# Grouping a front stage's small TensorE steps: four groups per chunk between the projection's units, instead of one step after nearly every unit

## What is computed

```python
u = x @ W_in + b_in                       # 8192 x 512 -> 8192 x 1536
uc = _short_conv(u, short_w, short_b)     # three taps along the sequence, per channel
x0, x1, v = jnp.split(uc, 3, axis=-1)
v = v * x1
k = _gen_filter(x.shape[1], W1, b1, f1, W2, b2, f2, W3, b3)   # sin(sin(pe @ W1) @ W2) @ W3, damped
v = _causal_fft_conv(v, k, filter_bias)
y = v * x0
return y @ W_out + b_out
```

## Time and profile before

| | us |
|---|---|
| median of 3 runs | 2255.05 |
| lowest and highest | 2248.68, 2259.68 |
| the profiled execution's own time | 2248.08 |
| its span | 2246.2 |

### The profile page before, as it was taken

How to read it: one execution, slowest core, us unless ns; L and a number is a source line. 1 busy time by engine, 2 the same in 40 slices (tenths; PEclk the granted TensorE clock), 3 DMA queues, 4 the chain that set the end, 5 groups by cost and what they waited for, 6 DMA issues and landing times. The chain is left out here.

```text
span 2246.2 us, 34847 instructions
## 1 busy us (share of the span) xinstructions
PE 1903.8 (85%) x12342; PEld 1293.3 (58%) x12342; DVE 1406.4 (63%) x2748; ACT 933.9 (42%) x1755; POOL 512.1 (23%) x410
## 2 busy tenths in 40 slices
PE   7999999999998799999979999995767586576444
PEld 6777777777776443443458888884636362352000
DVE  5877777877788454554558889884444353364344
ACT  4444444444444344454445555552323242242222
POOL 0100010001000054454445555550302020020000
PEclk9999999999999899999989999997888896697655
DMA  5134233433332577888778877774697999999999
GB/s 166 66 114 141 99 113 113 135 109 112 109 122 102 178 200 232 219 224 245 188 210 243 247 244 233 243 226 185 239 395 289 399 352 406 405 329 411 370 392 344
DMA packets 287298, 513.73 MB, mean 229 GB/s; under 512 B 26480, under 2 KB 105366, under 8 KB 278806
## 3 DMA queue, kind: packets, MB, share of 16 engines
q1 hardware_dynamic: 277909, 494.71, 65.6%
q10 hardware_dynamic: 9216, 16.78, 2.0%
HBM read 309.78 MB, written 201.62 MB: 228 GB/s over the span
## 5 line engine op out<-in xcount | busy, mean ns | idle before, releaser
L90 PE MATMUL p_pu<-p_xT_high,p_win_high 128*128 128x512 f32 (+1 forms) x816 | 330.8, 405 | 14.2 <-DVE p_win_low L85 11.9
L91 PE MATMUL p_pu<-p_xT_high,p_win_low 128*128 128x512 f32 (+1 forms) x816 | 314.4, 385 | 0.0
L92 PE MATMUL p_pu<-p_xT_low,p_win_high 128*128 128x512 f32 (+1 forms) x816 | 314.0, 385 | 0.0
L447 ACT ACTIVATE p_t<-p_pu,p_tbias,p_taps 128x512 f32<-128x512 f32 (+1 forms) x192 | 146.6, 764 | 357.9 <-PE p_pu L92 357.0
L564 DVE SCALAR_TENSOR_TENSOR p_t<-p_pu,p_taps,p_t 128x256 f32<-128x256 f32 (+1 forms) x384 | 208.6, 543 | 6.9
L85 POOL TENSOR_TENSOR p_xT_low<-p_xT,p_xT_high 128x2048 fp32r<-128x2048 f32 (+1 forms) x16 | 71.2, 4448 | 620.1 <-ACT p_xT_high L80 620.1
L849 POOL TENSOR_TENSOR q_y<-q_y 128x512 f32<-128x512 f32 x128 | 160.2, 1271 | 197.4 <-DVE q_y L870 197.4
L90 PEld LDWEIGHTS p_pu<-p_xT_high,p_win_high 128*128 128x128 f32 x816 | 156.4, 192 | 46.7 <-DVE p_xT_low L85 10.0
L92 PEld LDWEIGHTS p_pu<-p_xT_low,p_win_high 128*128 128x128 f32 x816 | 156.0, 191 | 32.8
L91 PEld LDWEIGHTS p_pu<-p_xT_high,p_win_low 128*128 128x128 f32 x816 | 156.4, 192 | 25.4
L1458 PE MATMUL e_pd<-e_taken,e_ff 128*32 128x128 f32 x2048 | 88.4, 329 | 96.0 <-DMA e_ff<-in_L_ffn_f 92.1
(11 more groups left out here) (135 smaller groups left out, 3782.2 us busy)
## 6 DMA issues: line engine op xcount, KB each, us to landing
s_I<-e_out SPq DMA_DIRECT2D x64, 1024.0 KB, 8.2
s_SV<-p_sout SPq DMA_DIRECT2D x128, 256.0 KB, 2.0
q_av<-s_SV SPq DMA_DIRECT2D x64, 512.0 KB, 4.4
s_Z<-q_z SPq DMA_DIRECT2D x128, 256.0 KB, 3.2
o_zin<-s_Z SPq DMA_DIRECT2D x64, 512.0 KB, 4.0
e_ff<-in_L_ffn_f SPq DMA_DIRECT2D x64, 512.0 KB, 9.4
e_inter<-s_I SPq DMA_DIRECT2D x32, 1024.0 KB, 12.3
e_taken<-s_I SPq DMA_DIRECT2D x32, 1024.0 KB, 11.5
```

Source lines behind the costliest of these rows:

```text
L90: pe.matmul(out, a[0], b[0], start=start, stop=False)
L91: pe.matmul(out, a[1], b[0], start=False, stop=False)
L92: return pe.matmul(out, a[0], b[1], start=False, stop=stop)
L447: nc.scalar.activation(t[r][m % 2][:, c], pu[(W + n) % 3][:, c], ACT.Identity, bias=tbias[:, w:w + 1], scale=taps[:, w, 2:3]).then_inc(t_o ...
```

## The change

PE's small steps of a pass no longer follow single units. They come in four groups, after units 2, 5, 8 and 11: two transform steps, one `turn_v`, and in three of the four groups one filter step (`filter_turn` of chunk i - 1 in the first, `filter_in` in the second, `filter_mid` in the fourth). The steps 0 to 5 of chunk i - 1 stand in the second to fourth group of pass i, its steps 6 and 7 in the first group of pass i + 1. On ACT and SP the copies and stores follow at x = 6, 7, 9, 10 and at 0, 1, 3, 4 of the next pass (`copied`). On DVE `angles(i, 0)` moves from x = 0 to x = 6, `angles(i, 1)` from x = 4 to x = 0 of the next pass, `keep_ht` and `keep_hs` to x = 2 of a later pass; on ACT `sine(i, 0)` moves from x = 2 to 8 and `sine(i, 1)` from x = 5 to x = 1 of the next pass, ahead of that place's `keep_s`. `filter_in` gets one more wait, for `ht_ok`. No instruction is added or taken away.

```diff
+        def copied(i, x):
+            ahead, back = {6: 0, 7: 1, 9: 2, 10: 3}, {0: 4, 1: 5, 3: 6, 4: 7}
+            if x in ahead and i >= 1:
+                return (i - 1) * STAGES + ahead[x]
+            return (i - 2) * STAGES + back[x] if x in back and i >= 2 else None
@@ SP
-                    if i and x == 1 and i >= 2:
+                    if x == 4 and i >= 2:
                         store_h(i - 2)
-                    if i and x >= 4:
-                        store_s((i - 1) * STAGES + x - 4)
+                    if copied(i, x) is not None:
+                        store_s(copied(i, x))
...
+            for n in range(NCH * STAGES - 4, NCH * STAGES):
+                store_s(n)
@@ PE, filter_in
                 if i:
                     pe.wait_ge(red2_ok, ONE + i)
+                    pe.wait_ge(ht_ok, ONE + i)
@@ PE
                 for x in range(W):
                     if i < NCH:
                         unit(i + 1, x)
-                        if x == 0:
-                            filter_in(i)
-                        if x == 3:
-                            filter_mid(i)
-                        if x == 7:
-                            filter_turn(i)
-                    m = i * DT + x // 3 - 1
-                    if x % 3 == 2 and 0 <= m < NCH * DT:
-                        turn_v(m)
-                    if i and x >= 4:
-                        stage(i - 1, x - 4)
+                    if x % 3 != 2:
+                        continue
+                    k = x // 3
+                    first = (i - 2) * STAGES + 6 if k == 0 else (i - 1) * STAGES + 2 * k - 2
+                    if first >= 0:
+                        stage(first // STAGES, first % STAGES)
+                        stage(first // STAGES, first % STAGES + 1)
+                    if 0 <= i * DT + k - 1 < NCH * DT:
+                        turn_v(i * DT + k - 1)
+                    if k == 0 and i:
+                        filter_turn(i - 1)
+                    if k == 1 and i < NCH:
+                        filter_in(i)
+                    if k == 3 and i < NCH:
+                        filter_mid(i)
+            for x in (6, 7):
+                stage(NCH - 1, x)
@@ ACT
                     if i < NCH:
                         tap(i, x)
-                        if x == 2:
+                        if x == 8:
                             sine(i, 0)
-                        if x == 5:
-                            sine(i, 1)
...
-                    if i and x >= 5:
-                        keep_s((i - 1) * STAGES + x - 5)
-                    elif i >= 2 and x == 0:
-                        keep_s((i - 1) * STAGES - 1)
-                if i == NCH:
-                    keep_s(NCH * STAGES - 1)
+                    if i and x == 1:
+                        sine(i - 1, 1)
+                    if copied(i, x) is not None:
+                        keep_s(copied(i, x))
+            for n in range(NCH * STAGES - 4, NCH * STAGES):
+                keep_s(n)
@@ DVE
-                if i >= 2:
-                    keep_hs(i - 2)
-                if i == NCH:
-                    break
                 for x in range(W):
-                    taps_add(i, x)
-                    if x % 3 == 2:
-                        gate(i * DT + x // 3)
-                    if x == 0:
-                        angles(i, 0)
-                    if x == 4:
-                        angles(i, 1)
-                    if x == 8:
-                        keep_ht(i)
+                    if i < NCH:
+                        taps_add(i, x)
+                        if x % 3 == 2:
+                            gate(i * DT + x // 3)
+                        if x == 6:
+                            angles(i, 0)
+                    if x == 0 and i >= 1:
+                        angles(i - 1, 1)
+                    if x == 2 and i >= 2:
+                        keep_hs(i - 2)
+                    if x == 2 and i >= 1:
+                        keep_ht(i - 1)
```

## The result

| | median | runs | lowest to highest |
|---|---|---|---|
| before | 2251.12 us | 19 | 2247.0 to 2259.68 |
| after | 2256.38 us | 19 | 2251.42 to 2263.17 |

The ratio is 1.0027, with a 95% interval of 1.0019 to 1.0035: the change costs 4 to 8 us, which is less than the 0.5% that was to count. The profiled execution of the changed kernel took 2260.33 us, with a span of 2258.5 us, where rows 1 gave 2246.2.

A forecast was written before the change was run, and what follows sets the result against it. PE's instructions were taken to bound the front up to about 700 us, then DVE. Terms 0 - 1.0 + 1.5 + 1.2 = +1.7 us on 2255.05 gave 2256.8 us, range 2247 to 2267.

The forecast's parts named there:

- The 0.09 is paid behind the short matmul whatever comes next: On PE, a step's 0.09 us on going out stays whether a unit or another small step follows.
- 8 x 0.00 for the pairs: On PE, putting transform steps in pairs saves nothing: 8 x 0.00 us a chunk.
- The first rival: The 0.09 us belongs to going back to units; seven exits a chunk go, -9.5 us, 2247; chance 0.15.
- The filter steps behind `turn_v` at 0: On PE, filter steps placed behind `turn_v`, a new kind of neighbour, cost 0 us extra.
- `filter_turn` at -0.07: On PE, `filter_turn` behind short transposes takes 0.22 us instead of 0.29: 15 x -0.07 = -1.0 us.
- The meeting of step 7 with the sine: First group of a pass: step 7's copy, behind the sine, allows 6.61 us after unit 0; PE arrives at 6.63.
- The +1.5 us for a bare weight load: Step 7's weight load in the first group is not hidden: 0.1 us, 15 times, +1.5 us.
- The other waits have slack: Mid-front waits other than step 7's are met in time, for example unit 0's additions at 2.7 us, needed at 8.5.
- DVE has 13.5 of 60 us free: In the middle of the front, DVE's 13.5 free us of 60 cover the bursts of additions.
- The end: Last gate at 746.3, 5.0 us earlier; chunk 15's first step 7.6 us later at 753.9 against 752.67: +1.2 us.
- The second: Rival: step 7 waits on the sine chain in every chunk, from 0.75 us each, 11.4 us slower; chance 0.15.
- the third rival: Only the end counts: DVE's waits stay and the clock falls again, +3.7 and up to 3 more, 2261 to 2262; chance 0.12.

The follow-up runs named there:

- experiment 7: Against experiment 4, each pair of transform steps split, one behind the second unit of three, the other behind the third: 2256.81 us, 1.0024 of before.
- experiment 1: Changed kernel with `angles(i, 0)` moved from x = 6 to 8 on DVE and `sine(i, 0)` from 8 to 10 on ACT: 2250.07 us, 0.9992 of before.
- experiment 4: Changed kernel with the filter chain back at its old places on every engine; steps, `turn_v`, copies and stores stay grouped: 2238.74 us, 0.9948 of before.
- experiment 8: The kernel of experiment 4 timed a second time, in another comparison with the kernel before: 2240.76 us, 0.9956 of before.
- Experiment 3: Changed kernel with, in the last pass on ACT, the copy of step 5 of chunk 14 ahead of `sine(15, 1)`: 2253.79 us, 1.0009 of before.
- experiment 5: Kernel before with only the filter chain moved to the changed kernel's places, steps left single: 2263.51 us, 1.0053 of before.
- the four kernels: Before, the changed kernel (1.0027 of before), grouping without the filter chain's move (0.9948), and the filter chain's move with single steps (1.0053).

## Why the prediction was right, and where it was wrong

The forecast, 2256.8 us and no change that counts, met the measured 2256.38. But before's median had moved down from 2255.05 to 2251.12 with more runs. The effect was +1.7 us by the sum and is 4 to 8 us by the ratio, 4.57 in the front by the traces. So that the two times agree within 0.4 us is luck. The direction and "no change that can be told" were right; the terms were not all.

- **"The 0.09 is paid behind the short matmul whatever comes next": wrong for the first step of a group.** The 1.08 us of rows 6 is the distance behind a step that itself follows a step. The *first* step behind a unit goes over in 1.02 to 1.03 us, into a step or into `turn_v` (experiment 7), so it pays 0.02 to 0.03 on going out. One exit in each of four groups is 0.26 us a chunk, about 4 us over 15 chunks, where the sum had 8 x 0.00 for the pairs and 0 for `turn_v` behind a step. The prediction had the number itself: it put step 6 at 1.03 us (T + 5.60 to T + 6.63) and named 1.03 as what would show it, but didn't carry the difference to 1.09 into the sum. The first rival had the sign right, not the size: one exit of a group goes, not all that no longer lead back to a unit.
- **The filter steps behind `turn_v` at 0, and `filter_turn` at -0.07: right.** In the kernel of experiment 1, without recurring waits, the four groups take 2.78, 3.37, 2.55 and 2.98 us from unit to unit: the 2.55 of two steps and `turn_v`, and 0.23 for `filter_turn`, 0.82 for `filter_in`, 0.43 for `filter_mid`. The prediction had 0.22, 0.83 and 0.44. That chunk takes 45.30 us against 45.58.
- **The meeting of step 7 with the sine: right to 0.02 us, its price not paid.** Timelines of ACT and PE, after, for a pass whose unit 0 ends at 438.15:

```profile
443.81 0.42 ACT L485 ACTIVATE p_h<-p_red 128x256 f32<-128x256 f32 x1 [1.61 <-DVE p_red L567]
444.13 0.57 ACT L479 COPY p_sout<-p_ps 128x512 f32<-128x512 f32 x1
...
444.78 1.10 PE L380 MATMUL p_ps<-p_shared,p_dft 128*128 128x512 f32 x2
```

  The sine is at T + 5.66 as forecast, the copy at T + 5.98, step 7 at T + 6.63, with no wait. The +1.5 us for a bare weight load is not there.
- **"The other waits have slack" and "DVE has 13.5 of 60 us free": the step that failed.** A mean over 60 us says nothing of one instruction of 0.29 us that takes 4.55. The hold stood in the trace of before (the rows at 416.70 and 418.47), and I didn't look at what DVE and POOL do at the place to which `angles(i, 0)` moves. It costs 0.46 us a chunk (45.76 against 45.30), 6 us in thirteen chunks. Whether the single wait of 2.4 us in pass 0 costs anything is not shown: experiment 1 has other waits in its place, and the start of the front differs by 1.7 us between two executions of one kernel (the last gate of chunk 0 ends at 74.61 in experiment 4, at 72.90 in experiment 8). The missed terms of the middle are of opposite sign (-0.26 and +0.46 a chunk), which is why the sum still came out near; that too is luck.
- **The end: the mechanism right, its sizes off.** The last gate was put at 746.3 and came at 748.7: the chunk before was 1.8 late at 710.78, where I had 709.0, and DVE took 37.95 to the next gate instead of 37.3, of which 0.5 was a wait for ACT. From the gate to the first step I had 7.6 us and it was 8.3: up to step 7 it is 3.8 (3.9 expected), but from step 7 to the first step of chunk 15 it is 4.5 (3.7 expected), at a granted clock of 0.50 (752 to 757 us). Together the first step came at 757.02, not 753.9: +4.4 against before instead of +1.2. Experiment 3 shows the part of the copy behind the sine in it, 3.6 us up to the first step.
- **Rivals and signs.** The second (the sine holds the first group, more than 0.75 us a chunk) did not arise in the middle. A wait that recurs in each chunk, which I named as what would prove me wrong, did, from another engine. So did a time outside the front that moved by more than 2 us (7.7), though only in the two profiled executions. Of the third rival the clock did fall, to 0.50 from 752 to 759 us, but DVE's waits did not stay. I had also called the filter chain's move nearly free, and by the four kernels it costs 12 to 18 us. What I judged neutral was one half that wins half a per cent and one that loses more.

## What to carry to other kernels

A change with two parts is costed, and if possible timed, as two: here a gain of 12 us and a loss of 18 were shipped together and looked like nothing. Where an instruction is moved to another place in a queue, look at that place in the trace for what the *other* engines do in those microseconds, above all GpSimd when VectorE's work moves; busy shares won't show it. And what ends a software pipeline has to be read apart: work that is put off into the next pass can be free in the middle and stands uncovered after the last pass, here 7.1 us from the last gate on.

## What the runs showed of the hardware

- A VectorE instruction that started 0.17 us after a GpSimd tensor-tensor on SBUF was held until 0.15 us behind its end: 4.55 beside 4.57 us, and 1.28 beside 1.30 once GpSimd's was cut to a quarter. Both a TENSOR_SCALAR (0.29 us alone) and a SCALAR_TENSOR_TENSOR of 128x128 (0.35 alone, 2.97 to 3.11 held) are hit. In every kernel here each VectorE instruction that started during this GpSimd instruction in the thirteen middle chunks ended 0.13 to 0.16 us behind it. ScalarE and PE showed nothing of the kind beside the same instructions: in experiment 5 ACT's copy at 420.90 takes 0.60.
- From the start of a transform step in fp32 (512 and 64 columns) it is 1.02 to 1.03 us to a small matmul behind it if a unit stands ahead of the step, 1.08 to 1.10 us if another step does, and a single step between units takes 1.09.
- A wait that PE records as 0.22 us cost 0.46 us, and one of 0.89 cost 1.09. In the first the weight load started 0.03 us ahead of its matmul instead of 0.23.
